# Causal attention on one NeuronCore: a ring of three PSUM banks for turned blocks and projections, and a new order of TensorE's work within a step

## The reference, cut to what matters

```python
x = x + layernorm(attention(layernorm(x)))      # 16 query heads, 4 key heads, head size 64
x = x + layernorm(ffn(layernorm(x)))            # linear, SwiGLU, top-4 of 8 experts + shared, linear, SwiGLU
def attention(h):
    q, k, v = h @ Wq, h @ Wk, h @ Wv            # q: 16 heads, k and v: 4 heads
    q, k = rope(q), rope(k)
    scores = where(causal, q @ k.T / 8, -1e30)  # 4 query heads share a key head
    return (softmax(scores) @ v) @ Wo
```

## Time and profile before

| | |
|---|---|
| median of 3 runs | 1554.12 us (1551.3 to 1555.63) |
| profiled execution | 1549.9 us, its span 1547.8 us |
| mean granted TensorE clock | 0.983 |
| attention | to about 1227 us of the span |
| feed-forward part | the rest |

### The profile page before, as it was taken

The page is one execution under the profiler, slowest core; times in us unless marked ns, Lnnn a source line. Parts: engine busy times, 40 slices in busy tenths (PEclk is TensorE's granted clock), DMA queues, the critical chain, the costliest instruction groups (busy, mean ns, idle before and its releaser), DMA issues.

```text
span 1547.8 us, 30949 instructions
## 1 busy us (share of the span) xinstructions
PE 1402.1 (91%) x10432; PEld 939.6 (61%) x10432; DVE 998.2 (64%) x2056; ACT 776.5 (50%) x1706; POOL 377.8 (24%) x388
## 2 busy tenths in 40 slices
PE   2799999988999999899999998999999899999997
PEld 1566666675666666766666666666666654444442
DVE  3576666845766768366767783767667557666665
ACT  2555565535555655355655553655555334333333
POOL 0333352113342520143524211424332000000000
PEclk9899999999999999999999999999999999999999
DMA  7202111011111110211110101110210000000000
GB/s 226 85 29 71 54 46 61 9 42 65 49 51 63 42 58 1 69 46 61 45 64 27 58 18 58 53 65 27 71 47 22 1 0 1 7 9 13 8 7 14
DMA packets 79027, 67.63 MB, mean 44 GB/s; under 512 B 39904, under 2 KB 62304, under 8 KB 78816
## 3 DMA queue, kind: packets, MB, share of 16 engines
q1 hardware_dynamic: 78944, 66.55, 13.2%
HBM read 7.81 MB, written 2.10 MB: 6 GB/s over the span
## 4 chain that ended last, share of the span: by engine, by line
PE 79%; DVE 9%; issue 5%; ACT 4%; SPq 2%; DMA 1%; POOL 0%; DVEq 0%; ACTq 0%; POOLq 0%
PE rows L419 19%; PE o_out L467 18%; PE turn L437 16%; PE rows L610 6%; PE rows L425 3%; PE o_out L633 3%; ACT probs L715 2%; PE o_out L387 2%; DVE neg_max L1043 2%; DVE probsT L1057 2%; PE proj_bank L387 1%; DVE ql L1035 1%; PE proj_bank L364 1%; PE turn L443 1%; PE proj_bank L366 1%
## 5 line engine op out<-in xcount | busy, mean ns | idle before, releaser
L1043 DVE TENSOR_REDUCE neg_max<-rows 128x1 f32<-128x768 f32 (+7 forms) x512 | 363.7, 752 | 279.4 <-PE rows L419 230.6
L715 ACT ACTIVATE probs<-rows,neg_max 128x768 f32<-128x768 f32 (+7 forms) x512 | 374.8, 738 | 236.0 <-DVE neg_max L1043 235.2
L437 PE MATMUL turn<-cf,probs 128*128 128x128 f32 x2304 | 348.3, 282 | 3.1 <-DVE probsT L1057 1.8
L467 PE MATMUL o_out<-probsT,v_g 128*64 128x128 f32 (+1 forms) x3328 | 305.8, 321 | 8.5 <-issue 6.5
L437 PEld LDWEIGHTS turn<-cf,probs 128*128 128x128 f32 x2304 | 255.2, 143 | 90.6 <-issue 77.0
L1057 DVE COPY probsT<-turn 128x512 f32<-128x512 f32 x384 | 258.9, 678 | 70.8 <-PE turn L437 70.4
L724 ACT ACTIVATE probsT<-turn 128x512 f32<-128x512 f32 x256 | 153.1, 598 | 238.3 <-PE turn L437 231.1
L467 PEld LDWEIGHTS o_out<-probsT,v_g 128*64 128x64 f32 x3328 | 197.6, 136 | 93.0 <-issue 50.3
L419 PE MATMUL rows<-kk,qh 64*128 64x512 f32 (+2 forms) x768 | 177.8, 459 | 71.1 <-DVE ql L1035 41.1
L911 POOL COPY inv_wide<-inv_sum 128x256 f32<-128x256 f32 x128 | 51.0, 399 | 781.8 <-DVE inv_sum L1049 692.0
L419 PEld LDWEIGHTS rows<-kk,qh 64*128 64x128 f32 x768 | 73.3, 187 | 135.0 <-ACT probs L715 84.5
(11 more groups left out here) (151 smaller groups left out, 1447.0 us busy)
## 6 DMA issues: line engine op xcount, KB each, us to landing
turned<-raw SPq DMA_DIRECT2D x192, 128.0 KB, 2.0
v_g<-v_all SPq DMA_DIRECT2D x32, 256.0 KB, 3.0
kk<-kk SPq DMA_DIRECT2D x16, 512.0 KB, 2.9
kl<-kl SPq DMA_DIRECT2D x16, 512.0 KB, 3.7
slab_a<-w_qk SPq DMA_DIRECT2D x16, 256.0 KB, 2.6
xm<-in_x SPq DMA_DIRECT2D x4, 512.0 KB, 7.3
slab_b<-w_qk SPq DMA_DIRECT2D x16, 128.0 KB, 2.2
out<-xm SPq DMA_DIRECT2D x8, 256.0 KB, 2.3
```

What stands on the lines that cost most here:

```text
L437: ins = nc.tensor.transpose(turn_bank[(s + j) % 2][:, (q - first) * 128:(q - first) * 128 + 128], probs[:, s % 2, q * 128:q * 128 + 128], ...
L467: ins = mm(dst, v_g[p][:, t, :], x, start=t == 0, stop=t == big_w - 1)
L715: A(probs[:, s % 2, q * 128:q * 128 + width], rows[h][:, 0:width], ACT.Exp, bias=neg_max[:, s % 2, item:item + 1], accum_out=exp_sum[:, s ...
L1043: V.tensor_reduce(neg_max[:, s % 2, item:item + 1], rows[h][:, 0:width], AX_X, ALU.max, negate=True).then_inc(max_ready, 1)
```

## The change

Three PSUM banks, the two of the turned blocks and `proj_bank`, become one `ring`; move j goes to `ring[j % 3]`. TensorE's step becomes: big scores, moves 0, 1, 2, all outputs, small scores, moves 3 and 4, projection. Move 2 goes to `proj_bank` and waits until ScalarE has copied the last projection out (`raw_kept`, count from the new `projected`); the projection waits for the copy of move 2. The masks of the big tile come behind both parts, and `rows_full` is always signalled by the mask matmuls. On ScalarE the copy of move 4 stands ahead of `keep_raw`. On VectorE the low part of the rotated piece stands ahead of the maxima of the small rows. At the end of a batch the first outputs of step 6 are no longer in front of the four projections but in `drain`.

```diff
--- before.py
+++ after.py
@@ -81,6 +81,11 @@
 def project_step(k):
 
     return 2 + k if k < PROJ_A else k - PROJ_A
+
+
+def projected(b, g, s):
+
+    return rope_index(b, g, PROJ_A + 1 + s if s < 2 else ROPES_G - 1 + min(s, PROJ_A + 1))
 
 
 def rope_plan(s, lag, last):
@@ -174,6 +179,7 @@
         rows = [ctx.enter_context(nc.psum_tensor(f"rows{h}", [128, S], F32)) for h in range(2)]
         turn_bank = [bank(f"turn{i}") for i in range(2)]
         o_out, proj_bank = bank("o_out"), bank("proj_bank")
+        ring = [*turn_bank, proj_bank]
         score = [rows[0][:, 0:HALF], rows[0][:, HALF:S]]
         block_max = [rows[1][:, 0:HALF], rows[1][:, HALF:S], turn_bank[0]]
         o_bank, m_bank = [o_out, turn_bank[1]], proj_bank
@@ -369,12 +375,6 @@
 
             def turn_tokens(b, a, dst):
 
-                if b and a == 0:
-                    pe.wait_ge(raw_kept, rope_index(b, 0, 0))
-                if b and a == 1 and b < B:
-                    pe.wait_ge(x_split, 2 * b + 1)
-                if a == 1 and b == B:
-                    pe.wait_ge(x2_kept, 1)
                 for t in range(4 * a, 4 * a + 4):
                     pe.wait_ge(ln_done, TILES * b + t + 1)
                     ins = nc.tensor.transpose(dst[:, t % 4 * 128:t % 4 * 128 + 128], x_norm1[:, t, :], ident)
@@ -393,8 +393,6 @@
                 n, c = k // 2, k % 2
                 if k in (0, PROJ_A):
                     pe.wait_ge(slab_a_in if k == 0 else slab_b_in, 16 * (b * HKV + g + 1))
-                if dst is proj_bank:
-                    pe.wait_ge(raw_kept, rope_index(b, g, k))
                 w = [slab_a[:, a, n * 128:n * 128 + 128] if k < PROJ_A else slab_b[:, a, :] for a in range(2)]
                 x = [xT[:, a, c * HALF:c * HALF + HALF] for a in range(2)]
                 split_product(dst[:, :], w, x, proj_done)
@@ -416,31 +414,32 @@
                     for n_pass, (q, k) in enumerate(((qh, kk), (ql, kk), (qh, kl))):
                         for h in range(2):
                             half = slice(64 * h, 64 * h + 64)
-                            ins = mm(rows[h][:, first:end], q[p][half, tile:tile + 128], k[p][half, first:end],
-                                     start=n_pass == 0, stop=n_pass == 2 and not first <= tile < end)
-                            if big and not first and n_pass == 2:
-                                ins.then_inc(rows_full, 1)
-                    if first <= tile < end:
-                        for h in range(2):
-                            ins = mm(rows[h][:, tile:tile + 128], identb, tri_q, start=False, stop=True)
-                            if not big:
-                                ins.then_inc(rows_full, 1)
-
-            def turn_probs(b, g, s, j):
+                            mm(rows[h][:, first:end], q[p][half, tile:tile + 128], k[p][half, first:end],
+                               start=n_pass == 0, stop=n_pass == 2 and not first <= tile < end)
+                for h in range(2):
+                    mm(rows[h][:, tile:tile + 128], identb, tri_q, start=False, stop=True).then_inc(rows_full, 1)
+
+            def turn_probs(b, g, s, j, at_last=False):
 
                 n = s % STEPS_P
                 sigma = step_index(b, g, s)
                 first, end = moves(n)[j]
                 pe.wait_ge(exp_done, 4 * sigma + max(item_of(n, q) for q in range(first, end)) + 5)
-                turn_kept(pe, *((sigma, j - 2) if j >= 2 else (sigma - 1, j + MOVES - 2)))
+                if j == 2:
+                    if at_last and s >= STEPS_G - 2:
+                        pe.wait_ge(x_split if b + 1 < B else x2_kept, (2 * b + 2 if b + 1 < B else 0) + s - STEPS_G + 3)
+                    elif not at_last or s < 2:
+                        pe.wait_ge(raw_kept, projected(b, g, s))
+                else:
+                    turn_kept(pe, *((sigma, j - 3) if j >= 3 else (sigma - 1, j + 3)))
                 for q in range(first, end):
-                    ins = nc.tensor.transpose(turn_bank[(s + j) % 2][:, (q - first) * 128:(q - first) * 128 + 128],
+                    ins = nc.tensor.transpose(ring[j % 3][:, (q - first) * 128:(q - first) * 128 + 128],
                                               probs[:, s % 2, q * 128:q * 128 + 128], ident)
                 if j == MOVES - 1:
                     pe.wait_ge(sum_spread, sigma + 1)
                     for big in range(2):
                         inv = inv_wide[:, s % 2, 2 - 2 * big:4 - 2 * big, :].rearrange("p h d -> p (h d)")
-                        ins = nc.tensor.transpose(turn_bank[(s + j) % 2][:, 256 + 128 * big:384 + 128 * big], inv, ident)
+                        ins = nc.tensor.transpose(ring[j % 3][:, 256 + 128 * big:384 + 128 * big], inv, ident)
                 ins.then_inc(turn_full, 1)
 
             def outputs(b, g, s, first, end):
@@ -474,23 +473,19 @@
                 g1, s1 = earlier(g, s, 1)
                 g2, s2 = earlier(g, s, 2)
                 if depth > 0:
-                    turn_probs(b, g1, s1, 0)
-                    turn_probs(b, g1, s1, 1)
+                    for j in range(3):
+                        turn_probs(b, g1, s1, j, last and s > 2)
                 if depth > 1:
-                    outputs(b, g2, s2, 0, 4)
-                if depth > 0:
-                    turn_probs(b, g1, s1, 2)
-                if depth > 1:
-                    outputs(b, g2, s2, 4, TILES)
+                    outputs(b, g2, s2, 0, TILES)
                 score_rows(b, g, s, 0)
                 if depth > 0:
-                    turn_probs(b, g1, s1, 3)
+                    for j in range(3, MOVES):
+                        turn_probs(b, g1, s1, j)
+                    turn_kept(pe, step_index(b, g1, s1), 2)
                 for ahead, k in rope_plan(s, 0, last):
                     project(b, g + ahead, k, proj_bank)
                 if last and s >= STEPS_G - 2:
                     turn_tokens(b + 1, s - STEPS_G + 2, proj_bank)
-                if depth > 0:
-                    turn_probs(b, g1, s1, 4)
 
             pe.wait_ge(consts_in, 32)
             pe.wait_ge(cb_ready, 1)
@@ -510,16 +505,15 @@
             def drain(b):
 
                 at = (b, HKV - 1, STEPS_G - 1)
-                turn_probs(*at, 0)
-                turn_probs(*at, 1)
-                outputs(b, HKV - 1, STEPS_G - 2, 4, TILES)
-                for j in range(2, MOVES):
+                for j in range(3):
+                    turn_probs(*at, j, True)
+                outputs(b, HKV - 1, STEPS_G - 2, 0, TILES)
+                for j in range(3, MOVES):
                     turn_probs(*at, j)
 
             def prologue(b):
 
                 if b:
-                    outputs(b - 1, HKV - 1, STEPS_G - 2, 0, 4)
                     pe.wait_ge(exp_done, 4 * step_index(b, 0, 0) + 4)
                 pe.wait_ge(x_split, 2 * b + 2)
                 for k in range(PROJ_A):
@@ -543,7 +537,6 @@
                 if b:
                     pe.wait_ge(wo_kept, 2 * b)
                 steps(pe, lambda *at: step(b, *at))
-            outputs(B - 1, HKV - 1, STEPS_G - 2, 0, 4)
             drain(B - 1)
             outputs(B - 1, HKV - 1, STEPS_G - 1, 0, TILES)
 
@@ -721,7 +714,7 @@
                 first = moves(s % STEPS_P)[j][0]
                 act.wait_ge(turn_full, MOVES * sigma + j + 1 + 2 * MOVES)
                 act.wait_ge(pv_done, sigma + 1)
-                A(probsT[:, s % 2, first * 128:first * 128 + HALF], turn_bank[(s + j) % 2][:, :], ACT.Copy
+                A(probsT[:, s % 2, first * 128:first * 128 + HALF], ring[j % 3][:, :], ACT.Copy
                   ).then_inc(kept_act, 1)
 
             def inverse_deviations(n, first, end):
@@ -757,12 +750,12 @@
                 if last and s == STEPS_P:
                     inverse_deviations(b + 1, 0, 2 * TILES if b else TILES)
                 exponentials(b, g, s, 0)
+                if depth > 0:
+                    keep_turned(b, *at, 4)
                 for ahead, k in rope_plan(s, 0, last):
                     keep_raw(b, g + ahead, k, proj_bank)
                 if last and s >= STEPS_G - 2:
                     keep_tokens(b + 1, s - STEPS_G + 2, proj_bank)
-                if depth > 0:
-                    keep_turned(b, *at, 4)
 
             act.wait_ge(consts_in, 32)
             A(cb[:], cb_raw, ACT.Copy).then_inc(cb_ready, 1)
@@ -1054,7 +1047,7 @@
                 first = moves(s % STEPS_P)[j][0]
                 dve.wait_ge(turn_full, MOVES * sigma + j + 1 + 2 * MOVES)
                 dve.wait_ge(pv_done, sigma + 1)
-                V.tensor_copy(probsT[:, s % 2, first * 128:first * 128 + HALF], turn_bank[(s + j) % 2][:, :]
+                V.tensor_copy(probsT[:, s % 2, first * 128:first * 128 + HALF], ring[j % 3][:, :]
                               ).then_inc(kept_dve, 1)
 
             def keep_outputs(b, g, s):
@@ -1080,11 +1073,11 @@
                     keep_turned(b, g1, s1, 2)
                 if depth > 1:
                     keep_outputs(b, *earlier(g, s, 2))
```

(4 more changed lines are left out.)

## The result

The changed kernel takes 1494.2 us (median of 4 runs, 1491.45 to 1495.79) against 1554.9 (4 runs, 1551.3 to 1559.9): a ratio of 0.961, interval [0.957, 0.964], 61 us less where 88 were forecast. All times and ratios are of undisturbed executions; one of the four of run 5 took 7352.6 us and is left out there.

A forecast was written before the change was run, and what follows sets the result against it. TensorE's own stream was taken to bound the kernel (busy 91% of the span). 32 + 19 - 8 + 17 + 15.5 + 5 + 8 = 88 us off the profiled 1549.9 gives 1462, as median 1466 us; range 1446 to 1502.

The forecast's parts named there:

- Products in one run: TensorE, big to small scores: one change to products and one away go, 0.33 us in 92 steps, 0.07 in 28: 32 us.
- Masks: Big tile's masks behind both score parts save TensorE 0.30 us per step, less where exponentials are late: 19 us, minus 8.
- the upper of the two bounds: Second part's first pass costs 0.23 like a pass after a pass, gain 0.30 us; the other bound: 0.34, gain 0.19.
- The low part in front: VectorE's low part ahead of small maxima, taking 0.68 us: starts of steps 4 and 0 gain 17, 15.5 and 5 us.
- The clock: Five of twelve starts after 1.75 us idle ran at lowered TensorE clock, 1.53 us each; all taken back: 8 us.
- The shared bank and the batch changes: Move 2's wait for the raw copy stays hidden by 0.4 to 0.6 us; batch changes 0, within 8 us either way.
- rival 3: Slower: move 2 waits for `keep_raw` in the 76 steps behind a projection, eating the 88 us or reaching 1580; chance 0.05.
- Rival 1: Small-row exponentials bind nearly everywhere, VectorE reaching the small maxima later; mask saving and half the products' lost: 1500 us; chance 0.14.
- Rival 2: The cost between TensorE stretches stays whatever the change of kind, so only the stalls pay: 1521 us; chance 0.08.

The follow-up runs named there:

- run 5: Kernel before with one part of the change alone, the masks of the big tile behind both parts: 1510.6 us (median of three), ratio 0.975.
- run 3: Changed kernel with the products in two runs around move 2 again: 1520.2 us, ratio 0.979.
- Run 1: Changed kernel, but GpSimd starts its sine product only when VectorE's low part of the piece before is done: 1456.8 us, ratio 0.938.
- Runs 6 and 7: Kernel before with the low part ahead of the small maxima: 1528.7 us, ratio 0.985; and the same with GpSimd's sine product waiting for it: 1508.3 us, 0.973.
- run 2: Changed kernel with VectorE's order as before, the low part behind the small maxima and the copy of move 3: 1492.2 us, ratio 0.961.

## Why the prediction came out as it did

- **Products in one run, 32 us: right in place and size.** M to N fell by 0.07, 0.34, 0.35, 0.34 for n = 0 to 3 (0.07 and 0.33 forecast), and in run 3 M to N gave 27 us back: 0.30 of the 0.34 are the products, the rest the transposes behind masks. At n = 0 the exponentials of 1024 columns bind, as said.
- **Masks, 0.30 us a step: right, and a little small.** Steps 0, 1, 4, 5 gained 0.28 to 0.30 from N to M'; the upper of the two bounds held. The 0.05 to 0.06 that the transposes gain behind masks lies in M to N and was missed (runs 3, 5).
- **The low part in front, priced at 0.68 us: the step that failed.** "So the exponentials need 1.8, 2.15, 2.38, 2.49 with a low part ahead" held for step 7 (2.37 us from N to the second part; the low part meets nothing there and takes 0.68) and failed for steps 2, 3 and 6: 3.15, 3.05 and 3.14. The mechanism forecast (what is late next is the exponentials of the small rows) is right; what was mis-sized is how late, because the low part met GpSimd's product, took 1.4 to 1.8 us, and was put at 0.68. 12 x (0.89 + 0.63 + 0.75) = 27 us, less 1.5 from step 7. Run 1 removes the meeting, at the price of a later GpSimd, and a group then takes 60.94 us, 0.4 under the forecast.
- **The clock, 8 us: only 2 or 3 of them won in the profiled run.** The five falls behind starts of step 0 are gone, but three came in other steps (231, 962, 1091 us), each behind a stall of 1.5 to 1.7 us after step 6, which was itself the work of the slow low part. They cost about 5 us.
- **The shared bank and the batch changes, 0: right.** TensorE never waits in front of move 2 for the raw copy within the groups, so rival 3 did not occur. From the last N of a batch to the first M of the next it took 45.7, 45.5, 45.5 us before and 46.0, 44.3, 45.9 after. Not foreseen: in three of the four last groups M to N of step 4 is 5.1 instead of 4.5 us. The trace shows a statistic of the layer norm (L956) ahead of VectorE's big maxima, which so start 0.79 us after M (557.84) instead of 0.10:

```profile
558.07 0.64 DVE L956 BATCH_NORM_AGGREGATE mean_var<-stats 128x2 f32<-128x6 f32 x8
558.63 2.32 DVE L1036 TENSOR_REDUCE neg_max<-rows 128x1 f32<-128x1024 f32 x2
...
562.26 0.39 PE L417 MATMUL rows<-kk,qh 64*128 64x256 f32 x2 [0.85 <-ACT probs L708]
```

In the kernel before the same work stood there, but TensorE came to step 4 later: it had waited 1.64 us for the low part. Runs 6 and 7, with the low part in front, have 5.2 us there too.

- **Rival 1** (VectorE late for the small maxima) describes what happened, in three steps of eight and for a reason that it did not name. Its 1500 lies nearer to the 1494 measured than my 1466. Rival 2 fell with runs 3 and 5.

88 - 25 - 5 - 2 for step 4 = 56; the two profiled executions differ by 54.3 us. The medians differ by 61, since the profiled execution of the kernel before was 5 us under its median and that of the changed kernel 1 over.

The Trainium skill, SBUF — State Buffer, Who interferes with whom, says that a VectorE instruction with two SBUF inputs contends with a GpSimd instruction that reads SBUF, and that the one that issues first holds the shared ports for the whole instruction. The trace agrees: in the 63 meetings of the changed kernel in which GpSimd started first, VectorE's low part ends 0.55 to 0.56 us after GpSimd's instruction (0.54 from the rounded rows), however much of that was left; and where VectorE is first, GpSimd's L895 takes 1.75 us instead of 1.28:

```profile
500.44 0.73 DVE L1028 TENSOR_TENSOR kl<-roped,kk 128x512 fp32r<-128x512 f32 x1
...
500.58 1.75 POOL L895 TENSOR_TENSOR turned<-turned,cf 128x512 f32<-128x512 f32 x1
```

VectorE's copies out of PSUM, whose only input is not in SBUF, keep at most 0.69 beside GpSimd's products. Applied to the order of the two queues in steps 2, 3 and 6, with the 27 us measured there, the forecast would have been near 1466 + 27 = 1493; that is an estimate made afterwards.

## What to carry to other kernels

When an instruction is moved on its queue, look at what the neighbour engines run at its new place: a duration read at a quiet spot is not its duration everywhere, and the spread from least to most in the trace (here 0.68 to 1.72 us for the same shape, in the kernel before already) says that something else decides it. If two engines exclude each other, let the one off the critical path wait by a semaphore; one line was worth 37 us of 1494 here (ratio 0.938 against 0.961). And changes between kinds of matmul (tile shapes) have a price that adds up: two fewer in a step of 8 us gave nearly 2% (run 3), and the masks in a place where they cost no change of their own some 2% more (run 5, without the clock).

## What the runs showed of the hardware that I had not expected

- The exclusion of VectorE's and GpSimd's element-wise products, in both directions, with the numbers above.
- The clock of TensorE does not follow the length of the idle time before it: in the kernel before, five of twelve starts after 1.75 us idle ran at a mean granted 0.65 over 4 us, that is at 1.2 GHz for much of it, and in run 5, with the same twelve waits of 1.75 us, none did, and in run 2 three; in the changed kernel three of the fourteen stalls of 1.5 to 1.7 us within the steps were followed by a fall. Four of the five in the kernel before are the starts of the four last groups, which hardly looks like chance; no run here shows what decides it. Some 8 us in 1550 depend on this.
- Eight float32 transposes take 0.97 us behind bf16 mask matmuls of the same tile shape and 1.03 behind scores of another.
